# Audio tower on one core: the last mixture layer computed over two lists of dispatched rows, and one wait of the first layer's convolution moved

## The reference, cut to what matters

```
def _L3_ffn_ref(x, Wg, W1, b1, W2, b2, ln_g, ln_b, out_g, out_b):
    xn = layer_norm(x, ln_g, ln_b)
    probs = jax.nn.softmax(jnp.einsum('bsd,de->bse', xn, Wg), axis=-1)
    top_p, top_i = jax.lax.top_k(probs, TOP_K)                # TOP_K = 2
    conf = top_p / top_p.sum(-1, keepdims=True)
    h = jax.nn.gelu(jnp.einsum('bsd,edh->bseh', xn, W1) + b1) # 128 -> 512, all 8 experts
    o = jnp.einsum('bseh,ehd->bsed', h, W2) + b2              # 512 -> 128
    sel = jnp.take_along_axis(o, top_i[..., None], axis=2)
    combined = jnp.einsum('bskd,bsk->bsd', sel, conf)
    return layer_norm(x + combined, out_g, out_b)
```

## Time and profile before

| | us |
|---|---|
| median of 3 runs (lowest, highest) | 3435.39 (3434.13, 3442.83) |
| the profiled execution | 3437.51 |
| its span, first to last instruction | 3435.7 |
| TensorE busy | 2910.1 (85%) |
| VectorE busy | 1768.1 (51%) |
| ScalarE busy | 1351.1 (39%) |
| GpSimd busy | 117.5 (3%) |
| mean granted TensorE clock, as share of 2.4 GHz | 0.896 |

### The profile page before, as it was taken

How to read it: one execution, slowest core, us unless ns; L and a number is a source line. 1 busy time by engine, 2 the same in 40 slices (tenths; PEclk the granted TensorE clock), 3 DMA queues, 4 the chain that set the end, 5 groups by cost and what they waited for, 6 DMA issues and landing times. The chain is left out here.

```text
span 3435.7 us, 46570 instructions
## 1 busy us (share of the span) xinstructions
PE 2910.1 (85%) x15629; PEld 1880.8 (55%) x15629; DVE 1768.1 (51%) x3628; ACT 1351.1 (39%) x2746; POOL 117.5 (3%) x152
## 2 busy tenths in 40 slices
PE   5399999999579996757887899999499999949997
PEld 3154444444368793424444456665366666637775
DVE  3366665565333615441334576776367767542223
ACT  2155555554213412224322355554145555524443
POOL 0000000000041050000000000000100000000000
PEclk8589999999689997878766899999699999968998
DMA  2344444443123610001000313221232322102110
GB/s 89 103 137 134 139 137 136 134 134 103 72 92 100 205 45 4 0 0 43 7 0 3 139 67 121 80 79 55 63 93 66 82 68 69 29 5 75 73 49 23
DMA packets 151157, 262.28 MB, mean 76 GB/s; under 512 B 44316, under 2 KB 114844, under 8 KB 146508
## 3 DMA queue, kind: packets, MB, share of 16 engines
q1 hardware_dynamic: 140580, 244.65, 22.7%
q10 hardware_dynamic: 7360, 9.44, 0.9%
q0 software_dynamic: 3072, 6.30, 0.6%
HBM read 153.80 MB, written 69.35 MB: 65 GB/s over the span
## 5 line engine op out<-in xcount | busy, mean ns | idle before, releaser
L2531 ACT ACTIVATE lstm_gate<-lstm_g_ps,lstm_bias 128x373 f32<-128x373 f32 x368 | 209.7, 573 | 250.3 <-PE lstm_g_ps L2492 235.6
L927 DVE TENSOR_REDUCE rel_nmax<-rel_s_ps 128x1 f32<-128x746 f32 x192 | 179.2, 933 | 195.3 <-PE rel_s_ps L784 150.8
L3130 DVE TENSOR_REDUCE caus_nmx<-caus_a_ps 128x4 f32<-128x512 f32 (+5 forms) x352 | 216.0, 642 | 106.1 <-PE caus_a_ps L2946 103.4
L891 ACT ACTIVATE rel_probs<-rel_s_ps,rel_nmax 128x746 f32<-128x746 f32 x192 | 169.6, 883 | 252.4 <-DVE rel_nmax L927 149.5
L2492 PE MATMUL lstm_g_ps<-lstm_state,lstm_w 128*128 128x373 f32 x640 | 253.8, 478 | 6.7 <-DVE lstm_state L2614 4.1
L3081 ACT ACTIVATE caus_probsT<-caus_s_ps 128x512 f32<-128x512 f32 (+4 forms) x352 | 189.7, 558 | 149.8 <-PE caus_s_ps L2965 146.1
L2486 PE MATMUL lstm_g_ps<-lstm_xm,lstm_w 128*128 128x373 f32 x512 | 202.3, 477 | 0.0
L1237 ACT ACTIVATE moe_hid<-moe_h_ps,moe_w 128x373 f32<-128x373 f32 x256 | 135.4, 572 | 144.8 <-PE moe_h_ps L431 144.8
L2946 PE MATMUL caus_a_ps<-caus_ks,caus_qs 96*128 96x128 f32 (+6 forms) x768 | 180.5, 327 | 10.4 <-DVE caus_nmx L3130 10.4
L2965 PE MATMUL caus_s_ps<-caus_qs,caus_ks 98*128 98x128 f32 (+6 forms) x768 | 186.2, 333 | 0.5 <-ACT caus_probsT L3081 0.4
L795 PE MATMUL rel_t_ps<-tower_ident,rel_probs 128*128 128x128 f32 x1152 | 167.0, 283 | 4.4 <-DVE rel_probsT L690 4.4
(11 more groups left out here) (445 smaller groups left out, 5469.6 us busy)
## 6 DMA issues: line engine op xcount, KB each, us to landing
lstm_row<-gates SPq DMA_DIRECT2D x16, 1536.0 KB, 13.9
moe_ew<-in_moe_w SPq DMA_DIRECT2D x33, 578.0 KB, 3.8
moe_gate<-gates SPq DMA_DIRECT2D x8, 1536.0 KB, 7.0
caus_qs<-caus_xh SPq DMA_DIRECT2D x128, 93.2 KB, 2.1
caus_ks<-caus_xh SPq DMA_DIRECT2D x128, 93.2 KB, 2.1
lstm_row<-gates SPq DMA_DIRECT2D x8, 1152.0 KB, 7.3
rel_shear<-rel_probs SPq DMA_DIRECT2D x32, 256.0 KB, 3.0
rel_bias<-rel_r_sb SPq DMA_DIRECT2D x32, 255.0 KB, 2.0
```

The lines of the kernel that those rows point to most:

```text
L891: nc.scalar.activation(probs[now.slot][:, t, 0:L], s_ps[t % 2][:, 0:L], ACT.Exp, bias=nmax[now.slot][:, t:t + 1], accum_out=sums[now.slot] ...
L927: nc.vector.tensor_reduce(nmax[now.slot][:, t:t + 1], s_ps[t % 2][:, 0:L], AX.X, ALU.max, negate=True).then_inc(max_ready, 1)
L2531: nc.scalar.activation(gate[x % 3][g][:], g_ps[n % RING][:, 0:HALF], ACT.Tanh if g == 2 else ACT.Sigmoid, bias=b[:, e, g:g + 1]).then_inc( ...
L3130: nc.vector.tensor_reduce(nmx[0:rows, slot, heads[0]:heads[-1] + 1, t:t + 1], heads_of(bank[0:rows, :], heads, k1 - k0), AX.X, ALU.max, ne ...
```

## The change

**Stage 8 is dispatched**, by a new function `listed_experts`, which takes the place of `plain_router`, `experts` and the block that added the kept input. It differs from stage 2's function in this: a token's first expert is one list and its second another, each list with its own DRAM tensors and room for 19 blocks of 256 rows (`LIST3`), 38 blocks in all (`NB3`). GpSimd scatters the first list (24 moves), then the second; it gathers the first list when that list's blocks are stored, and the second when all are. There is no convolution beside it. There is one pass of float32 matmuls in the first product and no split of operands. ScalarE applies gelu only; VectorE copies the transposed rows to SBUF and adds the bias. TensorE's first 32 blocks stand in a loop of 8 turns. The kept input is added where the results are transposed back.

**Stage 2** writes zeros over both lists' rows as well (66 + 38 rows per partition in five larger DMAs, in place of 66 in six), and its convolution no longer waits for `table_ready`: TensorE waits for `placed`, a signal that VectorE gives once the counts have been read from PSUM, ahead of the first `project`. The wait for `w_in` stays.

```
@@ conv_router @@
-            n = NB0 * SLOT // (P * ZERO_ROWS)
-            for i in range(n):
-                rows = xs[i * P * ZERO_ROWS:(i + 1) * P * ZERO_ROWS, :]
-                sp.dma_start(rows.rearrange("(p q) d -> p (q d)", q=ZERO_ROWS), zeros[:]).then_inc(xs_zero, 16)
-            sp.wait_ge(xs_zero, n * 16)
+            n = 0
+            for store, blocks in zip(xs, (NB0, LIST3)):
+                per = blocks * SLOT // P
+                rows = store.rearrange("(p q) d -> p (q d)", q=per)
+                for q in range(0, per, ZERO_ROWS):                     # ZERO_ROWS 11 -> 22
+                    cols = slice(q * P, min(q + ZERO_ROWS, per) * P)
+                    sp.dma_start(rows[:, cols], zeros[:, 0:cols.stop - cols.start]).then_inc(xs_zero, 16)
+                    n += 16
+            sp.wait_ge(xs_zero, n)
@@ sorted_experts @@
                 with pe.Fori(b0, b1) as b:
                     conv(b, 0)
                     conv(b, 1)
+                    pe.wait_ge(placed, 1)
                     project(b, 0)
                     project(b, 1)
...
             pe.wait_ge(w_in, 48)
-            pe.wait_ge(table_ready, 1)
             convolve(0, FIRST_B)
...
             c.link(nc.vector.tensor_tensor(place[:], counts[:, 0:TOK_TILES, :], base[:].unsqueeze(1).to_broadcast(full), ALU.add))
+            dve.sem_inc(placed, 1)
@@ new: listed_experts @@
+LIST3 = (TOK_TILES * P + E3 * (SLOT - 1)) // SLOT        # 19
+NB3 = 2 * LIST3
...
+            sp.wait_ge(table_ready, 1)
+            for n in range(BUFS):                              # BUFS = 4
+                load_weights(n)
+            for n in range(BUFS):
+                load_rows(n)                                   # rows 0 and 19 wait for scattered[k]
+            for n in range(NB):
+                if n + BUFS < NB:
+                    load_rows(n + BUFS)
+                store_rows(n)
+                if n + BUFS < NB:
+                    load_weights(n + BUFS)
...
+            for k in range(2):
+                for t in range(TOK_TILES):
+                    c = k * TOK_TILES + t
+                    pool.indirect_dma_start(xs[k], bass.IndirectOffsetOnAxis(ap=pos[:, c:c + 1], axis=0),
+                                            z_tok[:, t, :], None).then_inc(scattered[k], 16)
...
+            for k in range(2):
+                stored(pool, 0, (k + 1) * LIST3)
+                if k == 1:
+                    pool.wait_ge(s_full, NB)
+                for t in range(TOK_TILES):
+                    ...
...
+            for b in range(B):
+                for t in range(TILES):
+                    mm = nc.tensor.matmul(hb[b][:, t * E:(t + 1) * E], zT[:, at_col:at_col + P], wg[:], start=True, stop=True)
+                mm.then_inc(l_full, 1)
+            (24 transposes of zT to z_tok)
+            pe.wait_ge(marked, 1)
+            nc.tensor.matmul(counts, lower[:, 0, :], marks[:], start=True, stop=False)
+            for t in range(TOK_TILES):
+                (one matmul of 2 x (24 - t) x 8 columns)
...
+                if ahead:
+                    first(m * BUFS + n1, n1 % 2, n1 % BUFS, m * 16 + (n1 // BUFS + 1) * 16)
+                if beyond_n:
+                    turn(m * BUFS + n3, n3 % 2, n3 % BUFS, m * 16 + (n3 // BUFS + 1) * 16)
+                second(n, i % 2, i)
...
+            for n in range(NB):                                # VectorE
+                if n + 3 < NB:
+                    rows(n + 3)
+                output(n)
+            dve.wait_ge(first_back, TOK_TILES * 16)
+            for t in range(TOK_TILES):
+                (scale of the first list's rows by its gate)
...
+            mix(0)
+            for b in range(1, B):
+                mix(b)
+                add_kept(b - 1)
+            add_kept(B - 1)
@@ stage8 @@
-        plain_router(nc, io, K, "router3", E3, "wg3", None, gates_d, "sum")
-        z_parts = [a.sb(f"z_part{i}", [P, ZW], F32R)[:] for i in range(2)]
-        experts(nc, K, scratch, "moe3", E3, ACT.Gelu_apprx_tanh, io["moe3_w"], io["moe3_b2"], gates_d, y, z_parts)
-        (the block resid3: y += keep, 4 instructions on VectorE)
+        listed_experts(nc, io, K, keep, y, scratch["xs"], scratch["ys"])
```

More of the change, by code:

```diff
@@ L369, in audio_tower @@
         K["gathered"] = a.sems("gathered", B)
+        K["scattered3"] = a.sems("scattered3_", 2)
+        K["first_back"] = a.sem("first_back")
+        K["second_back"] = a.sems("second_back", B)
         load_constants(nc, io, K)
@@ L1299 @@
 NB0 = block_count(E0)
-ZERO_ROWS = 11
+ZERO_ROWS = 22
 def conv_router(nc, io, K, best, at, xs):
@@ L1446, in sorted_experts @@
         ys_out = a.sems("ys_out", Y_BUFS)
-        mixed, c_full, c_added, scaled0 = (a.sem(n) for n in ("mixed", "c_full", "c_added", "scaled0"))
+        placed, mixed, c_full, c_added, scaled0 = (a.sem(n) for n in ("placed", "mixed", "c_full", "c_added", "scaled0"))
         block = ctx.enter_context(nc.Block())
@@ L1814, in stage2 @@
 def stage2(nc, io, K, scratch):
-    xs = nc.dram_tensor("moe0_xs", (NB0 * SLOT, P), F32, kind="Internal").ap()
-    ys = nc.dram_tensor("moe0_ys", (NB0 * SLOT, P), F32, kind="Internal").ap()
+    xs, xs_b = (nc.dram_tensor(f"moe_xs{i}", (n * SLOT, P), F32, kind="Internal").ap() for i, n in enumerate((NB0, LIST3)))
+    ys, ys_b = (nc.dram_tensor(f"moe_ys{i}", (n * SLOT, P), F32, kind="Internal").ap() for i, n in enumerate((NB0, LIST3)))
+    scratch["xs"] = xs[0:LIST3 * SLOT, :], xs_b
+    scratch["ys"] = ys[0:LIST3 * SLOT, :], ys_b
     with ExitStack() as ctx:
@@ L1821, in stage2 @@
         at = a.sb("at", [P, TOK_TILES, 8], U32)
-        conv_router(nc, io, K, best, at, xs)
+        conv_router(nc, io, K, best, at, (xs, xs_b))
         sorted_experts(nc, io, K, best, at, y, xs, ys)
@@ L1843, in sort_layout @@
     return np.broadcast_to(row, (P, row.size))
-SORT_COLS = {E: E * SLOTS_MAX + E * E + block_count(E) * E + TOK_TILES * E for E in (8, 10)}
+SORT_COLS = {E0: E0 * SLOTS_MAX + E0 * E0 + NB0 * E0 + TOK_TILES * E0}
 def spread_scale(g):
@@ L1924, in stage8 @@
 def stage8(nc, io, K, scratch):
-    gates_d = nc.dram_tensor("gates3", (E3, B * LP), F32, kind="Internal").ap()
     with ExitStack() as ctx:
@@ L1940, in stage8, with sort_layout3 @@
         layer_norm(nc, K, "ln_in3", affine_d=(io["ln_in3_g"], io["ln_in3_b"]), src="zT")
-        plain_router(nc, io, K, "router3", E3, "wg3", None, gates_d, "sum")
-        z_parts = [a.sb(f"z_part{i}", [P, ZW], F32R)[:] for i in range(2)]
-        experts(nc, K, scratch, "moe3", E3, ACT.Gelu_apprx_tanh, io["moe3_w"], io["moe3_b2"], gates_d, y, z_parts)
[L1944 to L1954, removed]
+        listed_experts(nc, io, K, keep, y, scratch["xs"], scratch["ys"])
         layer_norm(nc, K, "ln_out3", src=y, affine_d=(io["ln_out3_g"], io["ln_out3_b"]), add=True)
 STAGES[8] = stage8
+SORT3_COLS = E3 * SLOTS_MAX + E3 * E3 + NB3 * E3 + TOK_TILES * E3
+def sort_layout3():
+    thresholds = np.broadcast_to(np.arange(SLOTS_MAX) * SLOT, (E3, SLOTS_MAX))
+    before = np.where(np.arange(E3)[None, :] < np.arange(E3)[:, None], SLOT, 0)
+    starts = np.broadcast_to((np.arange(NB3) % LIST3 * SLOT)[:, None], (NB3, E3))
+    iota = np.broadcast_to(np.arange(E3), (TOK_TILES, E3))
+    row = np.concatenate([v.reshape(-1) for v in (thresholds, before, starts, iota)]).astype(np.float32)
+    return np.broadcast_to(row, (P, row.size))
 def stage8_layout(f):
@@ L1963, in stage8_layout @@
         "wg3": f["L3_ffn_Wg"],
-        "moe3_w": expert_layout(f["L3_ffn_W1"], f["L3_ffn_b1"], f["L3_ffn_W2"]),
-        "moe3_b2": f["L3_ffn_b2"],
+        "moe3_w": np.concatenate([expert_layout(f["L3_ffn_W1"], f["L3_ffn_b1"], f["L3_ffn_W2"]),
+                                  np.broadcast_to(f["L3_ffn_b2"][:, None, :], (E3, P, P))], 2),
+        "sort3": sort_layout3(),
         "ln_in3_g": spread_scale(f["L3_ffn_ln_g"]),
```

275 lines of the change are left out of this document (added).

## The result

The changed kernel takes **3340.2 us**, the median of four runs (3337.7 to 3347.4), where the kernel before took 3436.5 beside it: a ratio of 0.9712, 95% interval 0.9695 to 0.9728, or 96 us less. The profiled execution took 3338.95 us with a span of 3337.1, against 3437.5 and 3435.7 before. The experiments ran in four later sessions, and in the first two of them every kernel took over 100 us longer (the kernel before 104 to 108, the changed one 155), so each run is compared with the kernel before of its own session.

The account below looks back on a forecast made before the run. Stage 8's dense loop keeps TensorE busy for all of its 289 us. Stage 8's -84.3 and stage 2's -6.6 sum to -90.9 on 3437.5, so 3346.6, median 3345 us; range 3330 to 3366.

Parts of the forecast that it names:

- Stage 2's wait: Stage 2: without the table's wait the convolution starts at 978.5 in place of 985.1, gaining 6.6 us.
- The zeros: Stage 2: the larger zero fill ends at about 932, hidden under 23 us of cover; uncovered it would cost 7 us.
- Head of stage 8: Stage 8 from logits through transposes, counting and ranking: first scatter at 3084.6, or 3078 less stage 2's 6.6.
- counting: Head of stage 8: 5200 columns, scaled from stage 2's 2.76 us for 3250, take 4.4 us.
- From the first scatter to the first `turn`: Stage 8: 29.5 us to the last of 24 scatter starts, 2.2 to landing, 2.8 for the row load.
- Block period: Stage 8's blocks: 4.15 us each over 37 periods, from a 4.01 loop through SyncE plus moves beside about 16 periods.
- rival of the crowded loop: Stage 8's blocks: moves crowd the row loads, 16 periods at 5.0 us, 13.6 us more: 3359; chance 0.12 to 0.14 group: 0.14.
- rival of TensorE's own pace: Stage 8's blocks: rows arrive in time, 3.73 us a block, 15.5 us less: 3329; chance 0.12.
- Tail: End of stage 8: 5.0 us to the second list's first gather, 24 gathers 1.25 apart, 4.8 us for mix, transposes, additions.
- 0.7 us for moves beside VectorE: Tail of stage 8: 0.7 us added for gathers beside VectorE's mixes; by the skill's rule it would be 4.8 us.
- The layer norm behind it is the same: Behind stage 8: the layer norm was taken as unchanged, with no time added for it.
- The clock: Stage 8's blocks: rival that TensorE stays at 1.2 GHz, 7.46 us a block, 122 us more: 3467; chance 0.04.

Follow-up runs that it names:

- e1: The kernel before with only stage 2's wait for the table moved behind the convolution's start: 3535.75 us against 3544.32, ratio 0.9981.
- e5: The changed kernel with the last layer's row loads issued one block earlier on SyncE, ahead of the weight load: 3482.2 us against the changed kernel's 3495.3.
- c2: The changed kernel with row loads ahead of weight loads in stage 2 and the last layer, and GpSimd's last waits there removed: 3313.8 us, ratio 0.9641.
- c3: c2 plus 32 matmuls that nothing reads, run on TensorE during the last gathers: 3317.9 us, ratio 0.9649 to the kernel before.
- a0: The changed kernel run again, unedited, in a slower session: 3495.3 us against 3540.8 for the kernel before, ratio 0.9870.

## Why the prediction was right

3345 us was predicted, 3340.2 measured, inside the range and on the side forecast. In the profiled execution's own terms 3346.6 stood against 3338.95. Point by point, with 6.6 taken off the places named for stage 8:

- **Stage 2's wait**, 6.6: the start came at 978.89 for 978.5, 6.2 earlier. Between there and the first gather (1210.7 for 1209.3) one more microsecond was lost; the longer stretch at 1.2 GHz is of that size, but no run tests it. e1 gives 6.7 for the part alone, 3.5 to 10. Right. The zeros were hidden, as priced.
- **Head of stage 8**: first scatter forecast at 3078.0, measured 3074.89. The mis-sized term is the counting, 4.4 us by scaling columns at the low clock's price; it took 2.4 (3067.99 to 3070.4), since TensorE had come up to speed on the logits and transposes: the granted clock is 1.00 from 3068 to 3071, where stage 2's counting, 962 to 966, had 0.50. The transposes took 5.1 for 5.8.
- **From the first scatter to the first `turn`**: 33.7 for 34.5; from there to the first `second` 7.6 for 8.0.
- **Block period**, 4.15 taken, 4.00 measured, 5.7 us over 37. The loop through SyncE that I had priced at 4.01 is what holds it without moves, 3.97, and e5 showed its cause by removing it. The mis-sized terms are two. Moves lay beside 12 periods, not 16, and these took 4.2 to 4.3 (5.0 in the rival of the crowded loop): some 3 us in all for the 5 priced (0.14 in each of 37). And the sum left out that the last three periods have less to do, 3.0 us each: 3 of the 5.7. The rival of TensorE's own pace (3.73) was wrong for this kernel; e5 reaches it in blocks without moves, and c2 in most of its blocks.
- **Tail**: last `second` to first list-2 gather 4.8 for 5.0; the gathers 1.25 apart; the last addition at 3304.2 for 3315.8 (11.6 early, 10 of them from above). The 0.7 us for moves beside VectorE was not needed: the slowest gather took 0.992 us. The Trainium skill, "SBUF — State Buffer", section "Who interferes with whom", has VectorE's copies, casts and scales block GpSimd only in their fast modes, and its instructions with two SBUF inputs contend only with a GpSimd instruction that reads SBUF; the prediction left out the second condition and priced every gather beside a scale or a mix. This trace shows no such stretch: gathers beside both took 0.94 to 0.99 us.
- **"The layer norm behind it is the same"** was the step that failed: 4.5 us more in front of it. The sum had no term for GpSimd's drain, though the trace of before held its row, hidden. c2 confirms it: its drain ends earlier against the last mix, and the wait is 1.76 us shorter.
- **The clock** stayed at 1.00 through the blocks, as I had weighted it. In the starved sessions it fell where TensorE got one matmul at a time (0.50 in e1 from 1020 to 1040 us). The Trainium skill, "TensorE: Matmul & The Clock Gate", section "HAM oscillation — how this bites in real kernels", says that short bursts of matmuls, each followed by a longer wait for data, fall back to the low clock; the trace agrees, though here the profile names nothing that is waited for.

From forecast to measurement: 3346.6 + 1.4 (stage 2) - 1.1 (won back between it and the logits, which start at 3052.82 for 3052.5) - 4.6 (head to first `second`) - 5.7 (blocks) - 1.6 (tail) + 4.5 (drain) - 0.5 (normalization) = 3339.0. The prediction was closer than its terms, and that was luck: the drain stood against the shorter head and blocks, and without it the miss would have been 12 us in place of 7.7. And it holds for sessions like the first: its range does not hold the time of the two starved ones (3495), nor did any rival name them.

## What to carry to other kernels

Where blocks wait a little for rows in each turn, look at what stands ahead of the row load in the issuing queue before blaming bandwidth: one load moved up on SyncE took 14 us from 33 blocks of stage 2 and 8 to 13 from 38 of the last layer. When a stage gets GpSimd's moves at its end, price GpSimd's drain as well, and look for its row where it is hidden now. And measure an overlap in more than one session: this one is worth 58 us in one kind and nothing in another.

## What was not expected of the hardware

- GpSimd's drain at the end of a program with indirect moves takes 7.89 to 7.90 us wherever a wait for their landing stands ahead of it, in stage 2 and in stage 8. Where none does (c2, c3), its record is 22.9 us long and ends 7.9 us behind the last issue. SyncE's takes 0.01.
- In two sessions, while GpSimd issued indirect moves, TensorE came down to a weight load and a matmul every 2.80 us, from 10 to 20 us behind the first move on (in a0's last layer, whose blocks start 34 us behind the first scatter, some 14 us into them), and ScalarE and VectorE stood still too, while the moves themselves took what they always took (0.96 us, 1.26 apart). It cost 50 us at each place where moves ran beside a convolution. The cause was not found; a chip with the same number did not show it later.
- Numbering a stage's semaphores in one run in place of six shortened the wait at its end by 0.3 us.
